# DLRM tower with CIN: the G product once a chunk, in four row quarters and four PSUM banks, with the work for the next chunk behind it

## The chip, the cores and the metric

The kernel runs on one core of a Trainium2 chip. The metric is the device time of the launch in microseconds, as the median of several runs.

## What is computed

39 embeddings of 16 numbers are picked for each of 512 samples; a compressed interaction network of three layers with 128 maps each runs on them; the sums of the three layers over the 16 numbers (z1, z2, z3) and a dense context go through a small MLP.

```python
def _cin_layer(X0, Xi, W, b):                     # X0 (512, 39, 16), Xi (512, Fi, 16)
    Wr = W.reshape(H, F0_, Fi)                    # H = 128
    return jnp.einsum('hjk,bjd,bkd->bhd', Wr, X0, Xi) + b[None, :, None]
X0 = embedded_features; Xi = X0; res = []
for W, b in Ws:                                   # three layers
    Xi = _cin_layer(X0, Xi, W, b)
    res.append(Xi.sum(axis=2))
z = jnp.concatenate(res, axis=1)
...
h = jnp.concatenate([z, dense_ctx], axis=1)
h = jnp.maximum(h @ W_top1 + b_top1, 0.0)
h = jnp.maximum(h @ W_top2 + b_top2, 0.0)
y = h @ W_top3
```

Of the third layer only the sum over d is needed. The kernel therefore forms G[k, j, b] = sum over d of X2[b, k, d] X0[b, j, d] for each sample, and layer 2 becomes 39 matmuls over G.

## The kernel before

The 8192 columns (sample, d) are worked off in 16 **chunks** of 512 columns (32 samples); a chunk has four **blocks** of 128 columns (8 samples). The engines run programs of their own, tied by semaphores, and each loops over chunks (`body`). Places in a chunk are written (i, g): block i, and g the group on PE (0 to 9), the place a among the six groups of ACT, or the place d among the four of DVE.

- **Layer 0** for chunk n + 1 runs in chunk n. SP loads shifted copies of x (`load_x`), ACT copies the rows to a PSUM bank (`store_rows`, rows_ps), DVE forms seven `products` (L481), and PE multiplies them by w0 into quad_ps (`layer0`, L630, seven times). ACT and DVE split the result into a high and a low half, x1_hi and x1_lo. PE also transposes x to xt (`transposes`, L634), in the same bank quad_ps.
- **Layer 1** (`layer1`, L679) has ten groups a block, each of four fields (group 9 of three) and three matmuls: 128 rows against 512 (or 384) columns. Groups 1, 4, 6, 9 go to two banks d_ps and are multiplied by xt and added up by DVE (L538). Groups 0, 2, 3, 5, 7, 8 go to three banks a_ps in turn and are scaled by ACT into `parts` (L902), which POOL adds pairwise (L303). DVE reduces what is left to x2t, the block of X2 with (sample, d) in the partitions (L550).
- **G** (`g_block`, L720): x2t of a block (128 rows) times `diag`, in which x stands on a block diagonal, one 40-column stripe for each of the block's 8 samples (39 fields and a column of ones, which gives z2). The result, 320 columns in g_ps, is copied by ACT to g_sb and z (`store_g`, L911, L912). diag is written by 16 DMAs a chunk from xt (`copy_diag`, L414), and by DVE for chunk 0 (L503).
- **Layer 2** (`layer2`, L733) runs in three parts over the stored G: in chunk 8, in chunk 15 and at the end. Then the MLP (L817, L826, L843, L848).

POOL also gathers the embeddings of chunks n + 2 and n + 3 (L277); SP writes them to x_rows (`write_x`, L373).

The order on each engine is written out by hand in tables of places. On PE, for example:

```python
L0_AT = {(1, 5): 0, (1, 7): 1, (2, 1): 2, (2, 3): 3, (2, 5): 4, (2, 8): 5, (3, 0): 6}
G_AT, STORE_G_AT = {(1, 9): 0, (2, 9): 1, (3, 9): 2}, {(1, 5): 0, (2, 5): 1, (3, 5): 2}
LAST_G_AT, STORE_LAST_G_AT = (1, 1), (1, 0)
```

G of block i is made behind group 9 of block i + 1, that of block 3 behind (1, 1) of the next chunk. Waits of G, of the transposes and of layer 0 are put on the second and third matmul of the layer 1 group ahead of them. Chunk 1 (`LATE`) and the chunks with a part of layer 2 (`PART_AT`) have tables of their own.

Of the kernel before, what the change touches and what calls it, by code (L numbers as in the profile page):

```python
# [24 lines left out]
CB = CW // D  # L25
# [3 lines left out]
BLKS = CW // 128  # L29

# [51 lines left out]
REDUCE_AT, FIRST_REDUCE_AT = 1, 2  # L82
HIGH_X1_AT, LOW_X1_AT, SUM_X1_AT, BIAS_Z1_AT = (3, 0), (3, 1), (0, 0), (1, 2)
PART_HIGH_X1_AT, PART_LOW_X1_AT = (3, 2), (3, 2)
LATE_HIGH_X1_AT, LATE_LOW_X1_AT = (3, 2), (3, 2)
PRODUCTS_AT = {(0, 3): (0,), (1, 0): (1,), (1, 2): (2,), (1, 3): (3,), (2, 0): (4, 5), (2, 2): (6,)}
LATE_PRODUCTS_AT = {(1, 0): (0,), (1, 2): (1, 2), (1, 3): (3,), (2, 0): (4,), (2, 2): (5,), (2, 3): (6,)}
FIRST_TILES = 4

ROWS_AT, LATE_ROWS_AT = (0, 5), (1, 0)  # L90
LATE = (1,)
# [5 lines left out]
FIRST_G_AT, FIRST_STORE_G_AT = {(2, 6): 0, (3, 2): 1, (3, 9): 2}, {(2, 4): 0, (3, 1): 1, (3, 5): 2}  # L97
# [29 lines left out]


def is_late(n):
    return isinstance(n, int) and n in LATE  # L130

# [10 lines left out]
def build(nc, picks0, picks, tables, x_first, x_rows, w0a, w0b, w1, w2, biases, b1_row, ctx_in, wt1, wt1c, bt1, wt2, bt2, wt3,  # L142
          ident_in, mask_in, out):
    with ExitStack() as stack:
# [32 lines left out]
        mask = sb("mask", [128, BLK_B])  # L177
# [31 lines left out]
        a_ps = [ps(f"a_ps{r}") for r in range(A_RING)]  # L209

# [19 lines left out]
        diag_copied = [sem("diag_copied_first"), sem("diag_copied_second")]  # L230
# [4 lines left out]
        g_ready, g_stored = sem("g_ready"), sem("g_stored")  # L235
# [105 lines left out]
        def _(sp):  # L341
# [96 lines left out]
            def body(n, u, w2_at=None, loading=True, writing=True):  # L438
                copy_diag(n, u, 0)
                copy_diag(n, u, 1)  # L440
# [8 lines left out]
            write_x(3, 0)  # L449
            body(1, 1, (0, W2_FIRST))  # L450
# [20 lines left out]
        def _(dve):  # L471
# [69 lines left out]
            def reduce_parts(n, i):  # L541
# [5 lines left out]
                if not (isinstance(q, int) and q < 2):  # L547

                    dve.wait_ge(g_ready, q - 1)
                nc.vector.tensor_reduce(x2t[:, i % 2, :], left[:, :, :], AX_X, ALU.add).then_inc(x2t_ready, 1)  # L550
# [17 lines left out]

            def body(n, u, last=False):
                late = is_late(n)  # L570
                low_x1_at = (PART_LOW_X1_AT if isinstance(n, int) and n in PART_AT else
                             LATE_LOW_X1_AT if late else LOW_X1_AT)
                products_at = LATE_PRODUCTS_AT if late else PRODUCTS_AT
                for i in range(BLKS):
                    for d in range(ND):
                        add_group(n, u, i, d)
                        if d == (FIRST_REDUCE_AT if i == 0 and isinstance(n, int) and n == 1 else REDUCE_AT):
# [8 lines left out]
                        if (i, d) == low_x1_at and not last:  # L586
                            low_x1(n + 1, 1 - u)
                        if not last:
                            for t in products_at.get((i, d), ()):
# [33 lines left out]
            reduce_parts(CHUNKS - 1, BLKS - 1)  # L623

        @block.tensor
        def _(pe):
# [31 lines left out]
            def layer1(n, u, i, g, transposing=False, starting=False, ending=False, g_of=None):  # L658
# [12 lines left out]
                else:  # L671
# [3 lines left out]
                    if a >= A_RING or not is_zero(q):  # L675
# [12 lines left out]
                elif g_of:  # L688

                    if is_zero(g_of[0]):  # L690
                        pe.wait_ge(first_diag, g_of[1] + 1)
                    else:
                        pe.wait_ge(diag_copied[g_of[1] // 2], 16 * BLK_B * g_of[0])
# [7 lines left out]
                if g_of:  # L701
# [367 lines left out]
```

## Time and profile before

| | before |
|---|---|
| time, median of 3 runs (lowest, highest) | 676.58 us (675.15, 676.62) |
| profiled execution | 681.37 us |
| its span, first to last instruction | 679.5 us |
| PE matmul busy / weight loads busy | 655.2 us (96%) / 480.9 us (71%) |
| DVE, ACT, POOL busy | 455.2 (67%), 478.7 (70%), 497.0 us (73%) |
| mean granted TensorE clock | 0.985 |

Busy is the union of an engine's instructions. Matmuls overlap one another in the records, so what one costs is read from the chain of waits, where each piece is the time from one start to the next. PE is TensorE's matmuls, PEld its weight loads. An fp32 matmul has two records and two loads; a transpose and an fp32r matmul have one. The clock is given as a share of 2.4 GHz.

### The profile page before, as it was taken

The page shows a single profiled execution, that of the slowest core. Times are in us where ns is not written, and L with a number is a line of the kernel's source. Part 1 is how long each engine was busy: PE and PEld are TensorE (multiplying, and loading weights), DVE is VectorE, ACT ScalarE, POOL GpSimd, SP SyncE. Part 2 cuts the span into 40 slices and gives each one's busy share as a digit, 9 for nine tenths or more (in the row PEclk, how much of TensorE's full clock was granted, in tenths as well). Part 3 has the DMA queues.
Part 4 walks back from the last instruction along what each step waited for, and adds up shares of the span by engine and source line. Part 5 has one row for each costly group of instructions (what it writes and reads, how often), then busy time and mean ns, then how long its engine had stood idle before and what let it go on. Part 6 is the DMA issues. An engine that isn't in the chain of part 4 may idle for free.

```text
span 679.5 us, 11233 instructions
## 1 busy us (share of the span) xinstructions
PE 655.2 (96%) x2680; PEld 480.9 (71%) x2680; DVE 455.2 (67%) x1180; ACT 478.7 (70%) x1735; POOL 497.0 (73%) x467
## 2 busy tenths in 40 slices
PE   3699989999999999999999999999999999999998
PEld 1386757777777777777787777777777777788563
DVE  1477757878686969687707677878686969674600
ACT  1466758878787879696907878878787879685502
POOL 5888967979797979888826797979797966563500
PEclk9989989999999999999999999999999999999889
DMA  6652514141514233241500515151413232002000
GB/s 157 150 112 54 120 26 116 33 122 13 121 32 104 49 90 61 61 92 39 114 6 5 116 13 118 13 118 13 111 18 90 39 67 57 4 4 83 1 1 0
DMA packets 68134, 43.18 MB, mean 64 GB/s; under 512 B 49418, under 2 KB 61645, under 8 KB 66329
## 3 DMA queue, kind: packets, MB, share of 16 engines
q1 hardware_dynamic: 56742, 37.91, 24.7%
q0 software_dynamic: 5184, 1.29, 2.3%
q10 hardware_dynamic: 6158, 3.45, 1.9%
q8 instruction: 15, 0.25, 0.2%
q14 instruction: 35, 0.29, 0.2%
HBM read 39.45 MB, written 1.96 MB: 61 GB/s over the span
## 4 chain that ended last, share of the span: by engine, by line
PE 88%; issue 3%; POOL 3%; DMA 2%; SPq 2%; DVE 1%; ACT 1%; POOLq 0%; ACTq 0%
PE a_ps L679 37%; PE d_ps L679 23%; PE quad_ps L630 12%; PE quad_ps L733 5%; PE g_ps L720 5%; POOL emb L277 1%; PE d_ps L817 1%; PE a_ps L843 1%; DMA emb<-tables_dram,rows_now 1%; DMA rows<-x_first 1%; POOL left L303 1%; PE quad_ps L634 1%; PE quad_ps L647 1%; SPq L414 1%; POOL parts L303 1%
## 5 line engine op out<-in xcount | busy, mean ns | idle before, releaser
L902 ACT ACTIVATE parts<-a_ps,xt 128x128 f32<-128x128 f32 x1536 | 423.3, 381 | 130.2 <-PE a_ps L679 116.6
L538 DVE SCALAR_TENSOR_TENSOR parts<-d_ps,xt,parts 128x128 f32<-128x128 f32 x704 | 201.7, 343 | 112.5 <-PE d_ps L679 104.6
L303 POOL TENSOR_TENSOR parts<-parts 128x512 f32<-128x512 f32 x128 | 163.4, 1294 | 103.3 <-ACT parts L902 102.5
L679 PE MATMUL a_ps<-w_hi,x_hi 128*128 128x512 f32 x384 | 181.7, 473 | 0.6 <-issue 0.6
L303 POOL TENSOR_TENSOR left<-parts 128x512 f32<-128x512 f32 x128 | 167.1, 1321 | 5.7 <-ACT parts L902 4.0
L277 POOL DMA_INDIRECT emb<-tables_dram,rows_now x150 | 144.2, 961 | 25.3 <-issue 18.8
L679 PE MATMUL a_ps<-w_hi,x_lo 128*128 128x512 f32 x384 | 152.5, 397 | 0.6 <-issue 0.6
L679 PE MATMUL a_ps<-w_lo,x_hi 128*128 128x512 f32 x384 | 151.7, 395 | 0.0
L679 PE MATMUL d_ps<-w_hi,x_hi 128*128 128x512 f32 (+1 forms) x256 | 126.5, 494 | 0.0
L630 PE MATMUL quad_ps<-products,w_sb 117*128 117x512 f32 (+1 forms) x210 | 107.8, 594 | 0.0
L679 PE MATMUL d_ps<-w_lo,x_hi 128*128 128x512 f32 (+1 forms) x256 | 97.7, 382 | 2.8 <-DMA diag<-xt 2.1
L679 PE MATMUL d_ps<-w_hi,x_lo 128*128 128x512 f32 (+1 forms) x256 | 97.2, 380 | 0.0
L550 DVE TENSOR_REDUCE x2t<-left 128x128 f32<-128x1280 f32 x64 | 94.6, 1477 | 2.1 <-POOL left L303 1.6
L679 PEld LDWEIGHTS a_ps<-w_hi,x_hi 128*128 128x128 f32 x384 | 72.5, 189 | 26.2 <-issue 8.7
L679 PEld LDWEIGHTS a_ps<-w_lo,x_hi 128*128 128x128 f32 x384 | 72.7, 189 | 24.5 <-issue 8.1
L679 PEld LDWEIGHTS a_ps<-w_hi,x_lo 128*128 128x128 f32 x384 | 72.5, 189 | 18.8 <-issue 1.2
L481 DVE TENSOR_TENSOR products<-shifted,rows_ps 117x512 f32<-117x512 f32 x105 | 70.2, 682 | 3.1 <-ACT rows_ps L890 3.1
L679 PEld LDWEIGHTS d_ps<-w_lo,x_hi 128*128 128x128 f32 x256 | 48.4, 189 | 28.3 <-issue 17.1
L679 PEld LDWEIGHTS d_ps<-w_hi,x_hi 128*128 128x128 f32 x256 | 48.2, 188 | 27.0 <-issue 11.9
L679 PEld LDWEIGHTS d_ps<-w_hi,x_lo 128*128 128x128 f32 x256 | 48.1, 188 | 8.5
L538 DVE SCALAR_TENSOR_TENSOR parts<-d_ps,xt,b_rows 128x128 f32<-128x128 f32 x64 | 22.4, 350 | 39.4 <-PE d_ps L679 27.8
L630 PEld LDWEIGHTS quad_ps<-products,w_sb 117*128 117x128 f32 (+1 forms) x210 | 40.1, 191 | 9.3
(67 smaller groups left out, 432.2 us busy)
## 6 DMA issues: line engine op xcount, KB each, us to landing
shifted<-x_rows SPq DMA_DIRECT2D x45, 312.0 KB
shifted<-x_rows SPq DMA_DIRECT2D x45, 234.0 KB
diag<-xt SPq DMA_DIRECT2D x240, 4.9 KB
rows<-x_rows SPq DMA_DIRECT2D x45, 78.0 KB
emb<-tables_dram,rows_now POOLq DMA_INDIRECT x150
w_sb<-w_dram SPq DMA_DIRECT2D x6, 384.0 KB
shifted<-x_first SPq DMA_DIRECT2D x12, 136.5 KB
g_sb<-w_dram ACTq DMA_DIRECT2D x2, 768.0 KB, 8.8
```

The source lines that it names most:

```text
L277: nc.gpsimd.indirect_dma_start(out=emb[0:parts, buf, g, :], out_offset=None, in_=tables[:, :], in_offset=bass.IndirectOffsetOnAxis(ap=rows ...
L303: nc.gpsimd.tensor_tensor(to, parts[:, i % 2, now:now + GF, :], parts[:, i % 2, more:more + GF, :], ALU.add).then_inc(pool_added, 1)
L414: sp.dma_start(diag[rows, blks, b, 0:FIELDS], xt[rows, u, blks, :]).then_inc(diag_copied[pair], 16)
L481: nc.vector.tensor_tensor(products[0:PK, t, :], shifted[0:PK, t, :], rows_ps[0:PK, :], ALU.mult).then_inc(products_ready, 1)
L538: nc.vector.scalar_tensor_tensor(now, d_ps[d % D_RING][:, H * at:H * (at + 1)], xt[:, u, i, j:j + 1], before, ALU.mult, ALU.add).then_inc( ...
L550: nc.vector.tensor_reduce(x2t[:, i % 2, :], left[:, :, :], AX_X, ALU.add).then_inc(x2t_ready, 1)
L630: nc.tensor.matmul(quad_ps[:, :], w0_sb[0:rows, t, :], products[0:rows, t, :], start=(t == 0), stop=(t == QT - 1)).then_inc(products_used, 1)
L634: return nc.tensor.transpose(bank[:, FIELDS * i:FIELDS * (i + 1)], rows3[0:FIELDS, 128 * i:128 * (i + 1)], ident[:, :])
L679: return nc.tensor.matmul(bank[:, 0:H * len(fields)], x[:, u, 128 * i:128 * (i + 1)], w[:, fields[0]:fields[-1] + 1, :].rearrange("p j h - ...
L720: nc.tensor.matmul(g_ps[:, 0:(FIELDS + 1) * BLK_B], x2t[:, i % 2, :], diag[:, i, :, :].rearrange("p b j -> p (b j)"), start=True, stop=Tru ...
L733: mm = nc.tensor.matmul(z3_ps[:, 0:(c1 - c0) * CB], w2_sb[:, j, :], g_sb[:, j, c0 * CB - base:c1 * CB - base], start=(j == 0), stop=(j == ...
L902: last = nc.scalar.activation(parts[:, i % 2, 2 + GF * a + at, :], a_ps[(NA * i + a) % A_RING][:, H * at:H * (at + 1)], ACT.Copy, scale=xt ...
```

## The change

G is made once a chunk, in the next chunk behind group (1, 0), for all four blocks (`make_g`). Each block's matmul of 128 rows and 320 columns becomes four of 32 rows and 80 columns: a quarter of 32 rows holds two samples, so only their two stripes of diag are needed, and diag shrinks from 8 to 2 stripes. Quarter r goes to a bank of its own: g_ps, quad_ps, rows_ps, a_ps1. The last is also one of layer 1's three banks, and group (1, 2) waits until it is copied. x2t is kept for four blocks. ACT copies quarters 1 and 2, DVE 3 and 0, each for the whole chunk; z2 is taken out of g_sb by one copy for each half of the samples. As quad_ps and rows_ps now hold G for a while, the rows, the transposes, the products and layer 0 move behind it. The tables for chunk 1 and for the chunks with layer 2 are gone. SP copies diag with 8 DMAs a chunk, and in chunk 1 before the write of chunk 3's first half. At the end the MLP uses d_ps0, d_ps1, a_ps0, a_ps2 instead of rows_ps, d_ps0, d_ps1, a_ps0.

```diff
+TILES = 4
+TILE_P = 128 // TILES
+TILE_B = BLK_B // TILES
-L0_AT = {(1, 5): 0, (1, 7): 1, (2, 1): 2, (2, 3): 3, (2, 5): 4, (2, 8): 5, (3, 0): 6}
-TRANSPOSE_AT, LATE_TRANSPOSE_AT = (0, 9), (1, 2)
-G_AT, STORE_G_AT = {(1, 9): 0, (2, 9): 1, (3, 9): 2}, {(1, 5): 0, (2, 5): 1, (3, 5): 2}
-LAST_G_AT, STORE_LAST_G_AT = (1, 1), (1, 0)
+L0_AT = {(1, 8): 0, (2, 0): 1, (2, 1): 2, (2, 3): 3, (2, 6): 4, (2, 9): 5, (3, 1): 6}
+TRANSPOSE_AT, STORE_XT_AT = (1, 3), (1, 1)
+LAYER2_AT, STORE_Z3_AT = (1, 6), (1, 3)
+G_AT, STORE_G_AT, VECTOR_STORE_G_AT = (1, 0), {(0, 5): 1, (1, 0): 2}, {(0, 3): (3, 0)}
+BEHIND_G = (1, 2)
+REDUCE_AT, FIRST_REDUCE_AT = 0, 2
+HIGH_X1_AT, LOW_X1_AT, SUM_X1_AT, BIAS_Z1_AT = (3, 1), (3, 2), (0, 0), (1, 2)
+PRODUCTS_AT = {(1, 1): (0,), (1, 2): (1, 2), (1, 3): (3,), (2, 0): (4,), (2, 1): (5,), (2, 2): (6,)}
+ROWS_AT = (1, 1)
...
+        g_banks = [g_ps, quad_ps, rows_ps, a_ps[1]]
+        def g_made(r):
+            return g_banks[r][:, 0:BLKS * TILE_B * (FIELDS + 1)].rearrange("p (i b j) -> p j i b", i=BLKS, b=TILE_B)
+        def g_kept(n, r):
+            kept = g_sb[:, :, n * CB % HB:n * CB % HB + CB]
+            return kept.rearrange("p j (i r b) -> p j i r b", i=BLKS, r=TILES)[:, :, :, r, :]
...
+            def copy_diag(n, u):
+                sp.wait_ge(xt_ready, transposed_now)
+                sp.wait_ge(g_ready, taken_before)
+                    sp.dma_start(diag[rows, :, b % TILE_B, 0:FIELDS], xt[rows, u, :, :]).then_inc(diag_copied, 16)
...
-            write_x(3, 0)
-            body(1, 1, (0, W2_FIRST))
+            body(1, 1, (0, W2_FIRST), first=True)
...
-                    if a >= A_RING or not is_zero(q):
+                    if (i, g) == BEHIND_G and not is_zero(n):
+                        pe.wait_ge(vector_stored, 2 * n - 1)
+                    elif a >= A_RING or not is_zero(q):
                         pe.wait_ge(staged_ready, NA * q + a - A_RING + 1)
...
-            def g_block(n, i):
-                q = BLKS * n + i
-                pe.wait_ge(x2t_ready, q + 1)
-                nc.tensor.matmul(g_ps[:, 0:(FIELDS + 1) * BLK_B], x2t[:, i % 2, :],
-                                 diag[:, i, :, :].rearrange("p b j -> p (b j)"),
-                                 start=True, stop=True).then_inc(g_ready, 1)
+            def make_g(n):
+                for i in range(BLKS):
+                    for r in range(TILES):
+                        rows, at = slice(TILE_P * r, TILE_P * (r + 1)), TILE_B * (FIELDS + 1) * i
+                        if i == 0 and r == 0:
+                            pe.wait_ge(x2t_ready, BLKS * (n + 1))
...
+                        mm = nc.tensor.matmul(g_banks[r][:, at:at + TILE_B * (FIELDS + 1)], x2t[rows, i, :],
+                                              diag[rows, i, :, :].rearrange("p b j -> p (b j)"), start=True, stop=True)
+                mm.then_inc(g_ready, 1)
...
-            banks = [rows_ps, d_ps[0], d_ps[1], a_ps[0]]
+            banks = [d_ps[0], d_ps[1], a_ps[0], a_ps[2]]
-                if mt == 1:
+                if mt == 0:
                     pe.wait_ge(vector_added, NDF * (last_q + 1))
-                elif mt == 3:
+                elif mt == 2:
                     pe.wait_ge(staged_ready, NA * (last_q + 1))
...
+            def store_g(n, r):
+                act.wait_ge(g_ready, n + 1)
+                nc.scalar.copy(g_kept(n, r), g_made(r)).then_inc(g_stored, 1)
```

Two places in the order of instructions. First TensorE's around (1, 0) and (1, 1) of chunk 9 (the first is chunk 0); before, one G (of block 3 of the chunk before) stood behind (1, 1), and the transposes ahead of (1, 0):

```order
799 L634 MATMUL quad_ps<-ident,rows 128x39 x4
800 L679 MATMUL a_ps<-w_hi,x_hi 128x512
801 L679 MATMUL a_ps<-w_lo,x_hi 128x512
802 L679 MATMUL a_ps<-w_hi,x_lo 128x512
803 L679 MATMUL d_ps<-w_hi,x_hi 128x512
804 L679 MATMUL d_ps<-w_lo,x_hi 128x512
805 L679 MATMUL d_ps<-w_hi,x_lo 128x512
806 L720 MATMUL g_ps<-diag,x2t 128x320
```

In the changed kernel the same place, behind group (1, 0), whose last row stands first here, holds four rounds over the four banks, rows 848 to 863, and then group (1, 1) from row 864. The first round and the start of the second:

```order
847 L693 MATMUL a_ps<-w_hi,x_lo 128x512
848 L750 MATMUL g_ps<-diag,x2t 128x80
849 L750 MATMUL quad_ps<-diag,x2t 128x80
850 L750 MATMUL rows_ps<-diag,x2t 128x80
851 L750 MATMUL a_ps<-diag,x2t 128x80
852 L750 MATMUL g_ps<-diag,x2t 128x80
853 L750 MATMUL quad_ps<-diag,x2t 128x80
```

So one matmul of 320 columns here, and three more elsewhere in the chunk, have become sixteen of 80 in one place, and the four transposes stand three groups further on.

Then ScalarE's in an ordinary chunk, from its rows copy behind (0, 5) to G of block 1, before:

```order
106 L890 COPY rows_ps<-rows 117x512
107 L902 ACTIVATE parts<-a_ps,xt 128x128 x4
108 L880 COPY xt<-quad_ps 128x156
109 L911 COPY g_sb<-g_ps 128x39x8
110 L912 COPY z<-g_ps 128x8
111 L902 ACTIVATE parts<-a_ps,xt 128x128 x20
112 L911 COPY g_sb<-g_ps 128x39x8
113 L912 COPY z<-g_ps 128x8
```

and in the changed kernel, from the groups up to (0, 5) to the xt copy behind (1, 1):

```order
74 L927 ACTIVATE parts<-a_ps,xt 128x128 x40
75 L937 COPY g_sb<-quad_ps 128x40x4x2
76 L927 ACTIVATE parts<-a_ps,xt 128x128 x4
77 L937 COPY g_sb<-rows_ps 128x40x4x2
78 L927 ACTIVATE parts<-a_ps,xt 128x128 x4
79 L915 COPY rows_ps<-rows 117x512
80 L904 COPY xt<-quad_ps 128x156
```

ACT's copies of G now come as two, a group apart, and the copies of rows and xt stand behind them.

## Rows read from the trace of the kernel before

**Rows 1.** Stretches: us, busy us (and instructions) of each engine, clock, DMA.

```profile
core 0: us, PE busy (x) PEld busy (x) DVE busy (x) ACT busy (x) POOL busy (x), PEclk, DMA share, GB/s
90.00:95.00 5.00, 3.17 (x8) 2.48 (x9) 2.13 (x6) 1.27 (x6) 4.65 (x5) 0.72 0.09 10
138.00:174.00 36.00, 36.00 (x148) 26.83 (x147) 27.96 (x75) 29.17 (x108) 30.68 (x30) 1.00 0.33 74
642.00:647.00 5.00, 5.00 (x6) 1.00 (x4) 0.17 (x1) 0.00 (x0) 0.00 (x0) 0.50 0.00 0
```

**Rows 2.** Chain of waits in mid-kernel: start us, us, what (x records).

```profile
141.90 0.54 PE g_ps L720 x2
...
157.45 0.37 PE quad_ps L634 x4
157.82 0.90 PE a_ps L679 x3
...
162.03 0.70 PE a_ps L679 x3
162.73 0.86 PE quad_ps L630 x2
...
166.55 0.53 PE d_ps L679 x3
...
193.78 0.89 PE a_ps L679 x3
```

**Rows 3.** Waits of PE from 33 us on: us in total, times, longest.

```profile
PE d_ps L679 <- DMA diag<-xt: 2.1, 1, 2.1
```

**Rows 4.** Groups of instructions: busy us, mean ns of one, idle before.

```profile
L720 PE MATMUL g_ps<-diag,x2t 128*128 128x320 f32 x128 | 45.9, 441 | 0.0
...
L902 ACT ACTIVATE parts<-a_ps,xt 128x128 f32<-128x128 f32 x1536 | 423.3, 381 | 130.2 <-PE a_ps L679 116.6 <-issue 11.5
L911 ACT COPY g_sb<-g_ps 128x312 f32<-128x312 f32 x64 | 29.0, 453 | 22.7 <-PE g_ps L720 22.6
...
L817 PEld LDWEIGHTS rows_ps<-z,shifted 128*128 128x128 f32 x6 | 1.0, 190 | 1.2 <-issue 1.2
...
L826 PEld LDWEIGHTS rows_ps<-shifted 16*128 16x128 f32 x2 | 0.3, 182 | 0.4 <-issue 0.4
```

**Rows 5.** Chain of waits: two parts of layer 2, and the end.

```profile
340.44 17.07 PE quad_ps L733 x78
...
608.96 8.71 PE quad_ps L733 x78
...
638.33 1.05 PE rows_ps L826 x2
...
651.20 1.02 PE g_ps L720 x2
```

**Rows 6.** Timeline of weight loads: start us, us to the last end.

```profile
84.21 0.19 PEld L679 LDWEIGHTS a_ps<-w_hi,x_hi 128*128 128x128 f32 x1
84.32 0.19 PEld L679 LDWEIGHTS a_ps<-w_lo,x_hi 128*128 128x128 f32 x1
...
157.38 0.26 PEld L634 LDWEIGHTS quad_ps<-ident,rows 39*128 39x128 f32 x3 [0.24 <-issue]
157.38 0.32 PEld L634 LDWEIGHTS quad_ps<-ident,rows 39*128 39x128 f32 x4 [0.24 <-issue]
```

**Rows 7.** Timeline of ACT in an ordinary chunk.

```profile
142.48 0.42 ACT L911 COPY g_sb<-g_ps 128x312 f32<-128x312 f32 x1 [0.45 <-PE g_ps L720]
...
158.28 0.65 ACT L890 COPY rows_ps<-rows 117x512 f32<-117x512 f32 x1
```

**Rows 8.** Timeline of SP, PE, PEld and DVE: chunk 1, and the last adds.

```profile
85.26 9.08 SPq L414 DMA_DIRECT2D diag<-xt  x14
91.83 0.45 PE L679 MATMUL d_ps<-w_lo,x_hi 128*128 128x384 f32 x1 [2.13 <-DMA diag<-xt]
96.01 0.19 PEld L679 LDWEIGHTS d_ps<-w_lo,x_hi 128*128 128x128 f32 x1 [0.24 <-issue]
...
638.36 0.71 DVE L538 SCALAR_TENSOR_TENSOR left<-d_ps,xt,parts 128x128 f32<-128x128 f32 x2
```

More of the change, by code:

```diff
@@ L126 @@
 W1_PART_AT = {0: 0, 3: 1, 6: 2}
-def is_late(n):
-    return isinstance(n, int) and n in LATE
 def is_zero(count):
@@ L546, in reduce_parts @@
                 dve.wait_ge(pool_added, ADDS * (q + 1))
-                if not (isinstance(q, int) and q < 2):
-                    dve.wait_ge(g_ready, q - 1)
-                nc.vector.tensor_reduce(x2t[:, i % 2, :], left[:, :, :], AX_X, ALU.add).then_inc(x2t_ready, 1)
+                if not is_zero(n):
+                    dve.wait_ge(g_ready, n)
+                nc.vector.tensor_reduce(x2t[:, i, :], left[:, :, :], AX_X, ALU.add).then_inc(x2t_ready, 1)
             def first_body():
@@ L567, in first_body @@
                             multiply_l0(1, t)
+            def store_g(n, r):
+                dve.wait_ge(g_ready, n + 1)
+                if n == HALF_CHUNKS:
+                    dve.wait_ge(z2_ready, 1)
+                nc.vector.tensor_copy(g_kept(n, r), g_made(r)).then_inc(vector_stored, 1)
             def body(n, u, last=False):
[L570 to L573, printed above, removed]
                 for i in range(BLKS):
@@ L585, in body @@
                                                     ).then_inc(z1_biased, 1)
-                        if (i, d) == low_x1_at and not last:
+                        for r in VECTOR_STORE_G_AT.get((i, d), ()):
+                            store_g(n - 1, r)
+                        if (i, d) == LOW_X1_AT and not last:
                             low_x1(n + 1, 1 - u)
                         if not last:
-                            for t in products_at.get((i, d), ()):
+                            for t in PRODUCTS_AT.get((i, d), ()):
                                 multiply_l0(n + 1, t)
@@ L623, in _ @@
             reduce_parts(CHUNKS - 1, BLKS - 1)
+            for r in (3, 0):
+                store_g(CHUNKS - 1, r)
         @block.tensor
@@ L931, in first_body, with body @@
                             store_xt(1, 1)
-                        if (i, a) in FIRST_STORE_G_AT:
-                            act.wait_ge(w1_lo_ready, 3)
-                            store_g(0, FIRST_STORE_G_AT[i, a], 0)
                         if (i, a) == SECOND_HIGH_X1_AT:
                             high_x1(1, 1)
-            def body(n, u, half, last=False, half_before=None):
+            def body(n, u, last=False):
                 part = PART_AT.get(n) if isinstance(n, int) else None
-                late = is_late(n)
-                high_x1_at = PART_HIGH_X1_AT if part is not None else LATE_HIGH_X1_AT if late else HIGH_X1_AT
                 for i in range(BLKS):
@@ L990, in _ @@
             first_body()
-            body(1, 1, 0)
-            for n in range(2, HALF_CHUNKS):
-                body(n, n % 2, 0)
-            body(HALF_CHUNKS, 0, 1, half_before=0)
-            body(HALF_CHUNKS + 1, 1, 1)
-            for n in range(HALF_CHUNKS + 2, CHUNKS - 2):
-                body(n, n % 2, 1)
-            body(CHUNKS - 2, 0, 1)
-            body(CHUNKS - 1, 1, 1, last=True)
-            store_g(CHUNKS - 1, BLKS - 1, 1)
+            for n in range(1, CHUNKS):
+                body(n, n % 2, last=n == CHUNKS - 1)
+            for r in (1, 2):
+                store_g(CHUNKS - 1, r)
+            store_z2(1)
             store_z3(2)
-            banks = [rows_ps, d_ps[0], d_ps[1], a_ps[0]]
+            banks = [d_ps[0], d_ps[1], a_ps[0], a_ps[2]]
             for mt in range(N1 // 128):
@@ L1008, in _ @@
                 act.wait_ge(mlp_ready, N1 // 128 + mt + 1)
-                nc.scalar.activation(h2[:, mt, :], a_ps[1 + mt][:, :], ACT.Relu, bias=bt2_sb[:, mt:mt + 1]
+                nc.scalar.activation(h2[:, mt, :], (a_ps[1], rows_ps)[mt][:, :], ACT.Relu, bias=bt2_sb[:, mt:mt + 1]
                                      ).then_inc(mlp_stored, 1)
```

150 lines of the change are left out of this document (71 added, 79 removed).

## Prediction

> **What bounds the kernel now.** I read the page's busy shares first: PE stands far above the other engines. Then the table of stretches, which shows PE busy for 36.00 of 36.00 us between 138 and 174 us at the full granted clock [rows 1], and the chain of waits, where the same point of two chunks lies 35.96 us apart (157.82 and 193.78) [rows 2]. The pieces of the chain add up to that by themselves: 36 groups of layer 1 at 0.70, 4 narrow ones at 0.53, seven products of layer 0 at 0.86, four G at 0.54 and the transposes, thus 25.2 + 2.1 + 6.0 + 2.2 + 0.6 = 36.1. So TensorE waits for nobody in an ordinary chunk, and a change is worth there what it does to PE's own time. The list of waits confirms it: in the chunks PE's longest wait is 2.1 us on the copy into diag, in chunk 1 [rows 3]. ACT and DVE have slack, but little: 29 and 28 of 36 us are filled [rows 1].
>
> **The change, part by part.** The sum is made on the profiled execution: 681.37 us, span 679.5. The median of the three timed runs is 676.58, 4.8 less. I take the difference found here off the median.
>
> *1. G itself.* Now: four matmuls of 128 rows and 320 columns, 0.54 us each, 2.16 us a chunk [rows 2]. Each is two records, with a weight load in each (128 records for 64 G) [rows 4]. New: 16 matmuls of 32 rows and 80 columns, so 32 loads and 32 matmul records. In columns nothing is saved, as 16 x 80 = 4 x 320. Only what runs at once can save, and no row of this trace shows two row quarters at work together. The bounds:
>
> - Streams. Layer 2 takes 17.07 us for 78 records of 256 columns and 8.71 for 78 of 128 [rows 5]: 0.219 and 0.112 us a record, 0.84 ns a column. 80 columns are 0.067 us, an instruction (two records) 0.133. All four quarters at once: 16 x 0.133 / 4 = 0.53 us. If only neighbouring instructions overlap, since the second record of one must follow its first in the same rows: 16 x 0.067 = 1.07.
> - Loads. Two full loads follow each other by 0.11 us (84.21, 84.32), the transposes' loads by 0.06 (a fourth one lengthens the piece from 0.26 to 0.32) [rows 6]. Fewer rows make a load no shorter: 182 ns for 16 rows, 190 for 128 [rows 4]. Loads in neighbouring quarters side by side: 16 x 0.112 = 1.79 us. All one behind the other: 32 x 0.112 = 3.58.
> - Changing the height of the array. The 16-row and 128-row matmuls that alternate after the last chunk take 1.05 us apiece at full clock [rows 5], layer 0's of the same 512 columns 0.86 [rows 2]: 0.19 a change. The transposes (39 rows) add 0.37 and stretch the next group from 0.70 to 0.90 [rows 2], 0.57 in all; less four load distances of 0.06 that leaves 0.33 for two changes. I take 0.35 for the two around G.
>
> I choose half way between the two neighbour bounds, 1.43 us, because the two records of an instruction must share their rows, and no row says whether streams or loads then set the pace; with 0.35 for the changes that is 1.78 us. Against 2.16 it is -0.38 a chunk, 16 chunks: **-6.1 us**. The ends are 0.53 + 0.35 = 0.88 (-20.5 us) and 3.58 + 0.35 = 3.93 (+28.3 us).
>
> The row above says that 16 rows load as slowly as 128. The Trainium skill has the same rule (TensorE: Matmul & The Clock Gate, "LDWEIGHTS (loading the stationary operand)"): a load costs its columns, not its rows. By that rule alone, with loads one by one, this change loses; that is the first rival. The skill's TensorEngine Tiling (Array Packing), "Tiling Modes", speaks for it: tiles load and multiply independently, and a change of mode drains the engine. No run here shows the first half yet; the 0.19 us of the rows agrees with the second. The first page's "Packing small matmuls — row/col tiling" also gives a measured 3.07x for four row quarters, an estimate of 2.16 / 3.07 = 0.70 us plus the changes.
>
> *2. G's copies.* Before: eight a chunk on ACT, the four large ones 453 ns in the mean [rows 4]. New: two on ACT and two on DVE of 320 elements, 0.45 to 0.5 us each. Both are covered by PE's work while they keep up, so they cost nothing themselves. The tight places, from T, the end of group 9 in block 0: (1, 0) ends at T + 0.70, G at T + 2.48. DVE empties a_ps1 first, by about T + 3.03; PE wants that bank for group (1, 2) at T + 3.18. ACT (four scaled copies of a group 1.10 us, 423.3 / 1536 x 4 [rows 4]; a copy of G began 0.04 us after its matmul, 141.90 + 0.54 [rows 2, 7]) does quadrant 1, group (1, 0), quadrant 2, group (1, 1), rows (0.65 [rows 7]), the short xt, group (1, 2), and is free at about T + 7.8; PE wants that bank for (1, 8) at T + 2.48 + 7 x 0.70 + 0.57 = T + 7.95. With so little room I allow 0.05 us a chunk, **+0.8**. After it, layer 0's own pieces of 0.86 us on PE give both engines time to catch up.
>
> *3. Order.* Transposes, rows, products and layer 0 come later in the chunk, in the same number, so PE gains or loses nothing. On SP the diag copies are 8 rather than 16 a chunk, and its loads of x are freed as before by the products of block 2 and meet a later user: no cost.
>
> *4. Chunk 1.* Before, SP has the write of x_rows for chunk 3, which waits for gathers, ahead of the diag copies; they start at 85.26, and PE waits 2.13 us for them in (1, 9) [rows 8]. Behind that wait the granted clock reads 0.72 [rows 1]; from 91.83 to 96.01 [rows 8] PE did what at full clock costs 2.44 us (0.35 + 0.53 + 0.70 + 0.86), a loss of 1.7. New: G of chunk 1 is wanted only in chunk 2, and the copies are issued before that write: **-3.8**. The smaller multiplies into diag in chunk 0 may bring a little more; I count nothing.
>
> *5. The end.* The first bank of the last layers is now d_ps0, which waits for DVE's last adds, over at 638.36 + 0.71 = 639.07 [rows 8], where rows_ps began at 638.33 [rows 5]: **+0.8**. The last G is four blocks behind the half-clock stretch (0.50) [rows 1], where one block cost 1.02 [rows 5]: streams and loads double, 2 x 1.43 + 0.35 = 3.21 against the 1.78 of part 1, less the 0.48 that the one block already lost: **+0.9**. Two large copies an engine rather than a large and a small one: **+0.3**.
>
> Sum: -6.1 + 0.8 - 3.8 + 0.8 + 0.9 + 0.3 = **-7.1 us**, thus 676.6 - 7.1 = **669.5 us**.
>
> **The rivals.** Parts 2 to 5 alone are -1.0; each rival adds its own G.
>
> - *Loads one after another (slower).* For it: loads cost by columns, and no row has two at once. Against: nothing in this trace. 3.93 a chunk: +28.3 - 1.0, 704 us. It decides once a load and its matmul take over (2.16 - 0.35) / 32 = 0.057 us on average; the full ones have 0.112.
> - *Break-even.* Quarters don't overlap, but their loads run at the transposes' 0.06: 32 x 0.06 + 0.35 = 2.3, +2.3 us; or the neighbour bound of loads holds, 1.79 + 0.35 = 2.14, -0.3 us. 675 to 678 us.
> - *All four quarters at once.* 0.88 us: -20.5 - 1.0, 655 us. Against: the two records of one instruction share their rows.
> - *A new stall or a lower clock.* ACT or DVE late by 0.5 us a chunk at (1, 2) or (1, 8) takes back 8 us: 677.5. Or a G of few rows makes the granted clock fall, as it had fallen by 642 us in matmuls that alternate 16 and 128 rows: at the 1.7 us of part 4, 16 times, +27, 697 us.
>
> **Numbers.** Partial overlap as forecast 0.38 (660 to 673 us), all at once 0.12, break-even 0.24, loads one by one 0.18, stall or clock 0.08. Within 0.3% (2 us) is what a measurement of this kernel can't tell from no change; of break-even half lies in there and a quarter on each side. Faster 0.38 + 0.12 + 0.06 + 0.01 = 0.57, same 0.12, slower 0.06 + 0.18 + 0.07 = 0.31. The range takes in 655, and above it the stalls and loads that overlap only in part: 654 to 698, leaving out most of the first rival.
>
> **What would show it.** Sixteen matmuls of 80 columns between (1, 0) and (1, 1), whose piece in the chain is 1.4 to 2.0 us, so that two records start within 0.06 us of each other on average; a chunk every 35.4 to 35.8 us; no wait of PE on diag; PE idle about 1.3 us before the last layers. Records 0.11 us apart and a chunk of 37.7 us mean the first rival. I am wrong too if PE waits at (1, 2) or (1, 8), or if the granted clock falls in mid-kernel.

## The result: 7.6% slower, and the profile after

The changed kernel takes 727.83 us (median of 4, 726.53 to 729.4), the kernel before 676.6 in the same session. The ratio is 1.076 with a 95% interval of 1.0719 to 1.0801. The forecast was 669.5 us with a range of 654 to 698. In some executions of a kernel, of before too, its last layers run at half clock for 10 to 20 us, in others not; that moves a time by some 9 us (e1 below took 679.1 us at a mean clock of 1.00 and 688.4 at 0.98), so I compare chunks as well as medians.

The page of the profiled execution (engines, and the slices in which the span is cut in 40):

```profile
span 724.6 us, 11784 instructions
PE 667.0 (92%) x3064; PEld 490.8 (68%) x3064; DVE 471.3 (65%) x1212; ACT 461.2 (64%) x1641; POOL 496.1 (68%) x467
PEclk9899999999989898989989989898998989999999
PE 44%; POOL 21%; issue 20%; ACT 8%; DVE 4%; DMA 1%; SPq 1%; POOLq 1%; DVEq 0%
```

TensorE's busy share is high, as before, but the last line, the chain by engine, says that it is no longer the bound by itself: POOL has 21% of the chain. And the granted clock dips again and again in mid-kernel. The stretches (columns as in [rows 1]) of two whole chunks, from one G to the next, and of the time right behind a G:

```profile
120.18:158.20 38.02, 35.34 (x174) 26.11 (x174) 28.90 (x77) 27.76 (x101) 30.59 (x30) 1.00 0.32 70
196.22:237.25 41.03, 38.35 (x175) 28.43 (x174) 28.95 (x77) 28.06 (x101) 30.60 (x30) 0.92 0.30 63
197.00:203.00 6.00, 6.00 (x38) 4.45 (x35) 3.41 (x7) 3.52 (x12) 2.73 (x3) 0.50 0.08 12
```

A chunk was 35.96 us [rows 2]. It is 38.02 now where the clock stays at 1.00, with 2.68 us in which PE is idle, and 41.03 where 6 us run at half clock. The waits between 100 and 650 us (us in total, times, longest):

```profile
POOL parts L309 <- ACT parts L927: 117.3, 56, 4.5
ACT g_sb L937 <- PE a_ps L750: 56.6, 13, 4.9
DVE x2t L555 <- POOL left L309: 47.4, 23, 3.2
PE d_ps L693 <- DVE parts L543: 32.5, 13, 2.7
```

The first two are idle time of engines that aren't the bound. The last two belong together, as the timelines of POOL, DVE and PE at the start of a chunk show:

```profile
185.17 1.29 POOL L309 TENSOR_TENSOR parts<-parts 128x512 f32<-128x512 f32 x1
186.61 0.96 POOL L283 DMA_INDIRECT emb<-tables_dram,rows_now  x1
187.59 1.32 POOL L309 TENSOR_TENSOR left<-parts 128x512 f32<-128x512 f32 x1
189.06 0.96 POOL L283 DMA_INDIRECT emb<-tables_dram,rows_now  x1 [0.15 <-issue]
190.03 1.32 POOL L309 TENSOR_TENSOR left<-parts 128x512 f32<-128x512 f32 x1
...
191.55 1.49 DVE L555 TENSOR_REDUCE x2t<-left 128x128 f32<-128x1280 f32 x1 [3.22 <-POOL left L309]
192.96 0.68 DVE L517 TENSOR_REDUCE z<-quad_ps 128x32 f32<-128x512 f32 x1
193.55 2.41 DVE L543 SCALAR_TENSOR_TENSOR parts<-d_ps,xt,parts 128x128 f32<-128x128 f32 x9
...
194.72 0.44 PE L693 MATMUL d_ps<-w_hi,x_hi 128*128 128x384 f32 x1 [2.68 <-DVE parts L543]
```

In the chunk's block 0, DVE comes to the reduce of the block before already behind its first group (REDUCE_AT = 0, before 1). It needs POOL's last add of that block, which ends at 191.35, because gathers of 0.96 us stand between the adds. DVE waits 3.22 us, and with it the adds that empty d_ps; PE waits 2.68 us for a bank at (0, 9). Then the clock falls. The same place in the timeline of the kernel before, which I had not looked at:

```profile
153.77 1.32 POOL L303 TENSOR_TENSOR left<-parts 128x512 f32<-128x512 f32 x1
...
153.13 0.68 DVE L512 TENSOR_REDUCE z<-quad_ps 128x32 f32<-128x512 f32 x1
154.17 1.13 DVE L538 SCALAR_TENSOR_TENSOR parts<-d_ps,xt,parts 128x128 f32<-128x128 f32 x4 [0.36 <-PE d_ps L679]
155.30 1.49 DVE L550 TENSOR_REDUCE x2t<-left 128x128 f32<-128x1280 f32 x1
```

POOL's add ends at 155.09, and the reduce begins at 155.30, in time by 0.2 us. Its new place is where `sum_x1` begins, at 153.13, 2.0 us too early.

G is the small thing that I argued most about. Its first matmuls (at half clock here):

```profile
196.15 0.50 PE L750 MATMUL g_ps<-diag,x2t 32*128 32x80 f32 x1
196.16 0.50 PE L750 MATMUL quad_ps<-diag,x2t 32*128 32x80 f32 x1
196.16 0.50 PE L750 MATMUL rows_ps<-diag,x2t 32*128 32x80 f32 x1
196.17 0.50 PE L750 MATMUL a_ps<-diag,x2t 32*128 32x80 f32 x1
196.44 0.42 PE L750 MATMUL g_ps<-diag,x2t 32*128 32x80 f32 x1
```

All four quarters start within 0.02 us: they do run at once. The starts of G near the end are a test that the kernel makes by itself. POOL's last gather starts at 598.1 us, so no gather stands between its adds of block 3 in chunks 13 and 14:

```profile
582.40 0.42 PE g_ps L750
...
620.87 0.26 PE g_ps L750
...
656.55 0.26 PE g_ps L750
```

The two stretches are 38.47 us and 35.68, where those before took 41.03. PE's wait at (0, 9) is 0.32 us at the end of each, and not 2.68; the first stretch still begins with a fall of the clock (0.57 from 581 to 589), behind the last long wait.

### The profile page after: what moved, and what is told of

It reads as the page before. It is cut to its first block, busy times and chain, and to the rows that moved or that the text cites. A ratio compares the mean times of both kernels' runs of the same rounds, so it can differ in the third digit from the quotient of the medians.

```text
span 724.6 us, 11784 instructions
## 1 busy us (share of the span) xinstructions
PE 667.0 (92%) x3064; PEld 490.8 (68%) x3064; DVE 471.3 (65%) x1212; ACT 461.2 (64%) x1641; POOL 496.1 (68%) x467
## 4 chain that ended last, share of the span: by engine, by line
PE 44%; POOL 21%; issue 20%; ACT 8%; DVE 4%; DMA 1%; SPq 1%; POOLq 1%; DVEq 0%
PE a_ps L693 15%; PE d_ps L693 11%; POOL left L309 9%; ACT parts L927 7%; POOL emb L283 6%; POOL parts L309 5%; PE quad_ps L764 5%; PE quad_ps L642 4%; PE g_ps L750 3%; DVE parts L543 2%; DVE z L517 1%; PE quad_ps L646 1%; PE d_ps L842 1%; PE a_ps L842 1%; DMA rows<-x_first 1%
## 5 line engine op out<-in xcount | busy, mean ns | idle before, releaser
L693 PE MATMUL a_ps<-w_hi,x_lo 128*128 128x512 f32 x384 | 157.4, 410 | 1.4 <-DVE x_lo L512 1.2
L693 PE MATMUL a_ps<-w_lo,x_hi 128*128 128x512 f32 x384 | 156.4, 407 | 0.0
L693 PE MATMUL d_ps<-w_hi,x_hi 128*128 128x512 f32 (+1 forms) x256 | 123.7, 483 | 32.8 <-DVE parts L543 32.8
L693 PE MATMUL d_ps<-w_lo,x_hi 128*128 128x512 f32 (+1 forms) x256 | 100.0, 391 | 0.2 <-ACT xt L904 0.2
L693 PE MATMUL d_ps<-w_hi,x_lo 128*128 128x512 f32 (+1 forms) x256 | 99.8, 390 | 0.0
L693 PEld LDWEIGHTS a_ps<-w_hi,x_hi 128*128 128x128 f32 x384 | 75.2, 196 | 29.5 <-issue 15.2
L693 PEld LDWEIGHTS a_ps<-w_lo,x_hi 128*128 128x128 f32 x384 | 75.3, 196 | 27.3 <-issue 14.7
L693 PEld LDWEIGHTS a_ps<-w_hi,x_lo 128*128 128x128 f32 x384 | 75.2, 196 | 20.1 <-DVE x_lo L512 1.6
L937 ACT COPY g_sb<-quad_ps 128x320 f32<-128x320 f32 x16 | 7.2, 453 | 69.0 <-PE a_ps L750 69.0
```

Source lines behind the costliest of these rows:

```text
L693: return nc.tensor.matmul(bank[:, 0:H * len(fields)], x[:, u, 128 * i:128 * (i + 1)], w[:, fields[0]:fields[-1] + 1, :].rearrange("p j h - ...
```

## The experiments

Theory R: the reduce, moved ahead of POOL's adds, makes the stall and the stall makes the clock fall. Its rival: the many small matmuls of G make the clock fall, or ACT waiting for them makes the stall; the expectations call it C, and G in e8. The table has all runs; "chunk" is the time between the same places of two chunks in mid-kernel (G, or the transposes where G is the old one) in the profiled execution. The ratio is to the kernel before as it ran in the same session.

| run | reduce behind group | two gathers of block 3 | else | chunk, us | median, us | ratio to before |
|---|---|---|---|---|---|---|
| before | 1 | in block 3 | | 35.96 | 676.6 | |
| changed | 0 | in block 3 | | 41.03, first 38.02 | 727.83 | 1.076 |
| e1 | 1 | in block 3 | | 36.53 | 688.12 | 1.014 |
| e3 | 1 in block 0, else 0 | in block 3 | | 36.85 | 688.12 | 1.016 |
| e5 | 1 | in block 3 | product 0 first | 36.09 | 681.76 | 1.006 |
| e6 | 1 | in block 3 | x1_lo earlier | 36.30 | 684.85 | 1.012 |
| e7 | 1 | in block 3 | both | 35.86 | 677.51 | 1.000 |
| e8 | 0 | end of block 2 | | 35.78 | 678.03 | 1.000 |
| e9 | 1 in block 0, else 0 | end of block 2 | | 35.07 | 667.79 | 0.980 |
| e10 | 1, block 3: 2 | end of block 2 | both, banks at the end | 35.29 | 670.24 | 0.984 |
| e4 | 1 | in block 3 | quarters in a row | 38.05, three 39.5 | 717.06 | 1.062 |
| e2 (before) | 0 | in block 3 | | 37.77, two 39.3 | 701.52 | 1.040 |
| e11 (before) | 1 | end of block 2 | | 35.96 | 675.5 | 0.993 |
| e12 (before) | 0 | end of block 2 | | 35.95 | 675.22 | 0.995 |

**e1, the reduce back.** The changed kernel with

```diff
-REDUCE_AT, FIRST_REDUCE_AT = 0, 2
+REDUCE_AT, FIRST_REDUCE_AT = 1, 2
```

> The changed kernel with DVE's reduce back behind its second group (REDUCE_AT = 1), all else as changed. Theory R (the early reduce holds DVE for POOL's last add, DVE keeps the d_ps banks, PE stalls at (0, 9) and its clock falls): no wait of PE on DVE, granted clock at 1.00 in mid-kernel, a chunk every 35 us, time 655 to 668 us. Rival C (the clock and the stall come from G itself: four banks held and ACT waiting 4 us a chunk for it): the stall stays or moves to (1, 2) or (1, 8), the clock still falls around G, time above 700 us. Rival P (POOL is too late whatever DVE does): PE still waits 1 to 2 us a chunk, 680 to 700 us.

Measured: 688.12 us (679.1 to 689.16), ratio 1.0139 (1.0087 to 1.0191). One number gives back 40 of the 51 us, and the clock, with G unchanged:

```profile
191.35:227.88 36.53, 35.61 (x174) 26.03 (x174) 28.56 (x76) 28.00 (x103) 30.55 (x30) 1.00 0.34 71
```

So the same G without the stall leaves the clock at 1.00: in this kernel the fall comes with the stall. The chunk is 4.50 us shorter, 1.49 of it at full clock (38.02 - 36.53) and 3.01 of it clock. But my theory was too hopeful: it said 655 to 668. The chunk is 36.53, above before. The time lies in the range of rival P, but PE doesn't wait for POOL, and DVE waits for it only 5.9 us in all. What is left shows in two waits of PE on DVE, one a chunk each:

```profile
PE a_ps L693 <- DVE x_lo L512: 7.2, 14, 0.5
PE quad_ps L642 <- DVE products L486: 4.9, 12, 0.4
```

**e2, the early reduce alone, in the kernel before** (REDUCE_AT = 0, nothing else).

> The kernel before with only the reduce moved ahead, behind DVE's first group (REDUCE_AT = 0). Theory R: the same DVE wait for POOL in block 0, PE waits 1 to 3 us a chunk on DVE and the clock falls, time 700 to 730 us. Rival C: with G as before nothing happens, 674 to 682 us.

Measured: 701.52 us, ratio 1.0403 (1.0344 to 1.0461). Half of the damage, with the old G. The chunk is 1.81 us longer than before at full clock (37.77 - 35.96), about as much as the stall costs in the changed kernel (1.49 against e1). What is missing is the clock: it was to fall in general, and it fell in two chunks, behind two of twelve waits of 1.5 to 1.6 us. PE waits 1.6 us at most instead of 2.7; the second fence is one of the two falls:

```profile
DVE x2t L550 <- POOL left L303: 33.9, 35, 2.1
PE d_ps L679 <- DVE parts L538: 18.6, 12, 1.6
```

```profile
121.00:126.00 5.00, 5.00 (x17) 3.81 (x18) 3.73 (x10) 2.01 (x8) 4.17 (x4) 0.66 0.12 13
```

**e3, the reduce back in block 0 only.**

```diff
-                        if d == (FIRST_REDUCE_AT if i == 0 and n == 1 else REDUCE_AT):
+                        if d == (FIRST_REDUCE_AT if i == 0 and n == 1 else 1 if i == 0 else REDUCE_AT):
```

> The changed kernel with the reduce moved back in block 0 of each chunk alone, which is the reduce of the block 3 before. Theory R in its narrow form (only that reduce meets POOL late, since POOL has gathers behind three adds of block 3): the same time as with all four moved back, within 2 us. Its wide form (every block's reduce is early): 5 us or more above it. Rival C: above 700 us.

Measured: 688.12 us, ratio 1.0158 (1.0078 to 1.0237), as e1. The stall at (0, 9) is gone with one reduce moved back, as the narrow form said. But the equal median isn't an equal kernel: the chunk is 36.85 against 36.53, DVE still waits for POOL 44.8 us, in 36 waits, almost three a chunk, and PE waits for the products 12.9 us. The lateness had moved, not gone.

**e4, the quarters in a row.** e1 with the loops of `make_g` exchanged, so that four matmuls in the same quarter follow each other.

```diff
-                for i in range(BLKS):
-                    for r in range(TILES):
+                for r in range(TILES):
+                    for i in range(BLKS):
```

> Reduce moved back, and the sixteen matmuls of G in the other order: all four blocks of quarter 0, then of quarter 1 and so on, so that neighbours share their 32 rows. If the four quarters run at once in the changed order (as its trace looks, eight rounds of 0.21 us at half clock), this order loses it: G takes 2.2 to 4 us instead of about 1.3, 15 to 40 us more than with the reduce alone moved back. If rounds were quick for another reason (short streams, cheap loads), the same time within 2 us.

Measured: 717.06 us, ratio 1.0619 (1.058 to 1.0658), 29 more than e1. The same 16 matmuls take 2.62 us, from 197.33 to 199.95, where in e1 they take 1.06, and the ordinary chunk is 1.52 us longer (38.05 against 36.53). The quarters don't run wholly one by one: each starts 0.51 us behind the last, which then has several records left, and the eight records of a quarter start 0.11 us apart. So the gain of e1's order lies in the alternation of the quarters.

Three chunks take 39.5 us instead of 38.05, because the clock falls behind G, in the first of them here:

```profile
161.00:165.00 4.00, 4.00 (x14) 2.81 (x13) 1.45 (x5) 3.46 (x13) 2.52 (x3) 0.57 0.11 15
```

No wait of PE in mid-kernel is longer than 0.53 us in this run. So the clock can fall without a long stall. That speaks for my rival that a G of few rows brings it down, for G in this order; in the changed kernel's order G leaves it at 1.00 in e1, e8 and e9.

**e5, e6, e7: the two waits left in e1.** All three start from e1. e5 puts the first product ahead of the reduce in block 1, e6 x1_lo one group earlier, e7 does both.

```diff
-PRODUCTS_AT = {(1, 1): (0,), (1, 2): (1, 2), (1, 3): (3,), (2, 0): (4,), (2, 1): (5,), (2, 2): (6,)}
+PRODUCTS_AT = {(1, 2): (1, 2), (1, 3): (3,), (2, 0): (4,), (2, 1): (5,), (2, 2): (6,)}
...
+                        if (i, d) == (1, 1) and not last:
+                            multiply_l0(n + 1, 0)
                         if d == (FIRST_REDUCE_AT if i == 0 and n == 1 else REDUCE_AT):
...
-HIGH_X1_AT, LOW_X1_AT, SUM_X1_AT, BIAS_Z1_AT = (3, 1), (3, 2), (0, 0), (1, 2)
+HIGH_X1_AT, LOW_X1_AT, SUM_X1_AT, BIAS_Z1_AT = (3, 1), (3, 1), (0, 0), (1, 2)
```

> The changed kernel with the reduce back behind the second group (as in the run reduce back), and in block 1 DVE makes the first of layer 0's products ahead of that reduce instead of behind it; nothing else. Theory W (what is left against the kernel before is made of two waits of PE on DVE a chunk, each because the reduce of 1.47 us now stands right ahead of a result that PE has no slack for): the first wait, of layer 0's first matmul at (1, 8), goes, PE quad_ps <- DVE products falls from 4.9 us to under 1 in 100 to 650, the chunk goes from 36.54 us to about 35.8, and the time from 688 to about 677. Rival H (PE's waits are only where a general lateness shows, since the products and the reduce are the same work in either order): the wait moves to d_ps or to the next product, and the time stays within 3 us of 688.

> The changed kernel with the reduce back behind the second group, and x1_lo of the next chunk one group earlier on DVE, at (3, 1) behind the reduce, where it stood in the kernel before; nothing else. Theory W: the second wait, of the third matmul of the next chunk on x1_lo, goes (PE a_ps <- DVE x_lo 7.2 us to 0 in 100 to 650, 0.5 to 0.7 us a chunk with what PE loses around it), the time falls by 7 to 10 us to about 680. Rival H: DVE's group (3, 2) is then later by 0.75 us, PE waits there for a bank of d_ps instead, and the time stays within 3 us of 688.

> Both edits of the two runs before it together: first product ahead of the reduce in block 1, and x1_lo at (3, 1). Theory W: the chunk is that of the kernel before less what G saves, 35.96 - 0.9 = 35.05 us, so 14 chunks give 12 to 13 us and chunk 1's wait on diag 4 more, less some us for the end of the kernel: 660 to 670, faster than the kernel before. Rival H: within 3 us of 688. Rival P (another bound stands close behind, that of DVE's adds or ACT's copies of G): between, 672 to 680, with new waits of PE on DVE parts or ACT parts.

Measured: 681.76, 684.85 and 677.51 us, ratios 1.006 (1.0012 to 1.0107), 1.0115 (1.0052 to 1.0179) and 1.0003 (0.9956 to 1.0051); the chunk goes from 36.53 to 36.09, 36.30 and 35.86. The savings add up (0.44 + 0.23 = 0.67), so the waits are two separate ones, each smaller than I had expected (0.7 and 0.5 to 0.7). e7 is rival P's case: a new wait stands close behind. It is there in e6 already, where rival H had it, with the same 4.0 us: the wait for x1_lo of 7.2 us is gone, and only 0.23 us a chunk is won.

```profile
PE d_ps L695 <- DVE parts L543: 4.0, 14, 0.3
```

**e8, the gathers early.** The changed kernel as it is, with

```diff
-GATHER_AT = (..., (2, 1), (2, 3), (3, 1), (3, 2), (3, 3))
+GATHER_AT = (..., (2, 1), (2, 3), (2, 3), (2, 3), (3, 3))
```

> The changed kernel as it is, the reduce behind the first group, with POOL's two gathers between its adds of block 3 moved to the end of block 2, where POOL idles 2.4 us for ACT; nothing else. Theory R (DVE's early reduce meets POOL's last add of block 3, and the adds are late because gathers of 0.98 us stand between them; PE's wait for a d_ps bank and the fallen clock follow from it): POOL ends those adds 1.9 us earlier, DVE x2t <- POOL falls from 47 us to under 25 in 100 to 650, PE's wait at (0, 9) from 2.7 to about 0.7 us a chunk, the clock of mid-kernel rises from 0.92, and the time falls from 728 to 695 to 710. Rival G (the clock falls because of G's 16 small matmuls, and DVE waits at all places alike): the clock stays at 0.92 to 0.95, and the time falls by under 10 us.

Measured: 678.03 us (669.65 to 678.58), ratio 1.0000 (0.9959 to 1.0042). One line of POOL's order takes 50 us off the changed kernel, more than the 18 to 33 that I expected. Now POOL issues three gathers in the time that it idled, and its adds follow each other:

```profile
178.58 0.94 POOL L283 DMA_INDIRECT emb<-tables_dram,rows_now  x1 [0.30 <-issue]
179.53 2.55 POOL L309 TENSOR_TENSOR parts<-parts 128x512 f32<-128x512 f32 x2
182.04 2.56 POOL L309 TENSOR_TENSOR left<-parts 128x512 f32<-128x512 f32 x2
...
184.80 1.49 DVE L555 TENSOR_REDUCE x2t<-left 128x128 f32<-128x1280 f32 x1 [0.99 <-POOL left L309]
```

```profile
189.47:225.25 35.78, 35.33 (x175) 26.10 (x174) 28.93 (x77) 27.76 (x101) 30.45 (x30) 1.00 0.34 74
```

The second fence is the stretch of a chunk. DVE's wait of 3.22 us is 0.99 (27.6 us in all, not under 25), PE's of 2.68 is 0.5 at most, and the clock no longer falls in mid-kernel, with G as it was.

**e9, gathers early and the reduce of block 0 back.** Both edits, of e8 and of e3.

> The changed kernel with POOL's two gathers moved to the end of block 2 (as in the run gathers early) and, in block 0 alone, the reduce behind the second group. Theory R2 (what waits in the run gathers early, 0.5 us a chunk of PE at (0, 9) with 0.2 to 0.3 around it, comes from block 0, where DVE waits for POOL 1.3 us and then has the reduce and sum_x1 ahead of its second group): that wait goes, the chunk goes from 35.78 to about 35.2 us, the time from 678 to about 670. Rival D (the reduce at (0, 1) pushes DVE's product 0 at (1, 1), as it did without the gathers' move): PE quad_ps <- DVE products comes back with over 5 us in 100 to 650, and the time is 675 to 685.

Measured: 667.79 us (666.05 to 668.47), ratio 0.9801 (0.9709 to 0.9894). This beats both kernels, and by theory R2's numbers; rival D's wait for the products isn't there. PE works without a gap, and the chunk is what G alone should make of it, 35.96 - 0.90 = 35.06 (the 0.90 is worked out from the pieces of the chain further down). The stretch of a chunk, and in a second fence the start of it in the chain (the rest of G's rounds left out):

```profile
185.76:220.84 35.08, 35.08 (x175) 26.19 (x174) 28.82 (x76) 27.82 (x103) 30.52 (x30) 1.00 0.35 74
```

```profile
185.76 0.26 PE g_ps L750
...
186.82 0.90 PE d_ps L693 x3
187.72 1.40 PE a_ps L693 x6
...
220.84 0.26 PE g_ps L750
```

**e10, the other way there.** e7 with the gathers early, block 3's reduce one group later still, and at the end ACT's two banks ahead of DVE's two.

```diff
-                        if d == (FIRST_REDUCE_AT if i == 0 and n == 1 else REDUCE_AT):
+                        if d == (FIRST_REDUCE_AT if i == 0 and n == 1 else 2 if i == 3 else REDUCE_AT):
...
-            banks = [d_ps[0], d_ps[1], a_ps[0], a_ps[2]]
+            banks = [a_ps[0], a_ps[2], d_ps[0], d_ps[1]]
```

> The run with both edits (reduce behind the second group, product 0 ahead of it in block 1, x1_lo at (3, 1)) with three more: POOL's two gathers at the end of block 2, block 3's reduce behind its third group, and at the end of the kernel ACT's two banks taken ahead of DVE's two. Theory W: PE's last waits of the middle (PE d_ps <- DVE parts 4.0 us in 100 to 650) go, the chunk comes near 35.96 - 0.9 = 35.1 us from 35.86, and PE's 4.6 us wait ahead of the last layers becomes about 1 to 2: the time goes from 677.5 to 660 to 667, faster than the kernel before. Rival P (some other engine bounds the chunk near 35.8): the chunk stays at 35.7 to 35.9, and only the end gives 3 us: 674.

Measured: 670.24 us, ratio 0.9838 (0.9746 to 0.9929), chunk 35.29; theory W's time was 660 to 667. The wait on d_ps is gone; 0.22 us more than in e9 stay, and where is open. The 4.6 us that the expectation takes for a wait ahead of the last layers was a misreading: it is the time from where the chain leaves PE to the first of the last layers (635.83 to 640.43 in e1), and for most of it PE still works. PE's wait is 1.3 us in e1 and e7 and 1.1 in e10, so there was little to win.

**e11 and e12, the same order in the kernel before.** e11 moves only the gathers, e12 the gathers and the reduce (to group 0).

> The kernel before with POOL's two gathers at the end of block 2, as a control of the run gathers early. Theory R: POOL is no one's wait in the kernel before (DVE x2t <- POOL 1.6 us in all), so nothing changes: within 2 us of the kernel before. Rival K (the gathers' place is worth something by itself, and the 50 us of that run are not the meeting of reduce and POOL): faster by over 5 us.

> The kernel before with the reduce behind the first group (as in the run before, reduce early, 701.5 us) and POOL's two gathers at the end of block 2. Theory R (an early reduce is dear only where it meets POOL's gathers, whatever G is like): most of the 25 us comes back, DVE x2t <- POOL from 35.6 us to under 15 in 100 to 650, the time from 701.5 to 678 to 685. Rival E (the early reduce is dear by itself, since the adds of POOL end late in any case): 693 to 702.

Measured: 675.5 us for e11, ratio 0.993 (0.9886 to 0.9974). The kernel before had a median of 683.03 beside e9 to e11, with more of its ends at half clock, and 676 to 677 elsewhere; its chunk and that of e11 are the same, so I take this for no gain, and count e9 and e10 against 676 to 677 as 1.0 to 1.4% faster. That is cautious: all times of e9 and e10 have a mean clock of 0.979 to 0.985, and the times of before at such a clock beside them are 681.8 to 685.5 us, which makes them about 2% faster. e12 takes 675.22 us, ratio 0.9952 (0.9917 to 0.9986): with the gathers out of the way, the early reduce that cost 24 us costs nothing. DVE still waits for POOL 17.6 us in all (33.9 in e2; I had expected under 15), but PE no longer waits for DVE. That is the cleanest test of the stall in theory R, since G is the old one; it says little of the clock, which fell only twice in e2.

## Why the prediction was wrong

**The step that failed is part 3, "Order".** It said that transposes, products and layer 0 "come later in the chunk, in the same number, so PE gains or loses nothing". I counted instructions and not the waits between them, and I never looked at two numbers of the diff: REDUCE_AT from 1 to 0, and LOW_X1_AT from (3, 1) to (3, 2) (worth 0.23 us a chunk in e6). The trace of before would have told: POOL's add ended 0.2 us ahead of the reduce that needs it, so a reduce one group earlier had to wait. In the changed kernel that cost, up to the end of layer 1, 686.24 - 618.02 = 68.2 us against e9: a stall of 2.95 us (38.02 - 35.07) in eleven chunks, 32; 3.0 us of lost clock in ten, 30; the remaining 6 stand ahead of chunk 2's G (4.6) and in chunks 13 and 14. That half of it is clock I know from rows (0.92 against 1.00), and that it goes with the stall from e1 and e8. What a stall needs to bring the clock down stays open: the first two of twelve waits of 2.68 us had no fall behind them, two of twelve waits of 1.6 us in e2 had one, and in e4 the clock fell three times with no wait over 0.53.

**Part 1, G, was right in direction and too timid in size.** I took half way between bounds, 1.43 + 0.35 us. The chain of e9 has G at 1.06 (185.76 to 186.82) and 0.20 more in the next group, 1.26 in all, -0.90 a chunk instead of -0.38. The rival "all four quarters at once" (0.88) was right in its mechanism: a round of four starts every 0.11 us at full clock, 0.21 at half. Eight rounds are 0.9, so 0.36 is left for the two changes of height, forecast at 0.35. The 0.11 is the distance of two full loads in [rows 6], not the 0.067 of an 80-column stream, and in e4 the records of one quarter are 0.11 apart as well. So each quarter keeps this pace by itself, and four keep it side by side; that it is the loads that set it I only conclude from the equal distance. The objection that the two records of one matmul share their rows counts for nothing: two records are two rounds. With 32 records / 4 x 0.11 + 0.35 the sum would have been 1.23.

The Trainium skill (TensorEngine Tiling (Array Packing), "Tiling Modes") says that tiles load and multiply in parallel; the runs agree (1.06 us for e1's order, 2.62 for e4's). The Trainium skill's 3.07x for four row quarters (TensorE: Matmul & The Clock Gate, "Packing small matmuls — row/col tiling") isn't reached: 2.16 / 1.06 is 2.04, and 1.7 with the change of height. The two aren't quite the same ratio: its streams have 512 columns, these have 80, and 2.16 is the time of the full-height matmuls. Against the same small matmuls quarter by quarter, which overlap in part, it is 2.62 / 1.06 = 2.5.

**Part 2, the copies**, was right in kind: in the changed kernel and in e9 PE doesn't wait at (1, 8); at (1, 2) PE's loads wait 2.2 us in 14 chunks in e9 for DVE's copy, 0.16 us a chunk, partly under PE's work. So the copies cost between nothing and 2.2 us, against the +0.8 of the sum.

**Part 4, chunk 1**, was right in kind: no wait on diag remains. e9 is through with group (1, 0) of chunk 2 at 115.63, the kernel before at 121.87 + 0.89 = 122.76: 7.1 us ahead. Of that 2.2 are only put off, since before had by then made three G of chunk 1 (1.62) and the transposes (0.57), which e9 makes later. Of the other 4.9 I had forecast 3.8 for the wait and its clock and 0.4 for chunk 0's G, which gave 0.9. The changed kernel is only 2.6 us ahead there, as the first stall stands in between.

**Part 5, the end.** The wait for d_ps0 was forecast at 0.8 and is

```profile
687.37 1.09 PE L851 MATMUL d_ps<-shifted 16*128 16x512 f32 x2 [1.15 <-DVE left L543]
```

1.15 us. The rest depends on the clock: in this execution the last layers run at full clock, and from layer 1's end the kernel takes 36.2 us (686.24 to 722.47) against 39.0 before (638.33 to 677.33); in that of e9, where 620 to 637 stands at 0.51, 45.4. Where the reduce stands matters little here: PE waits 1.28 us at this place in e1 and 1.30 in e7, with the reduce at group 1, and 1.15 in e8 and e9.

**The rivals and the numbers.** The last rival, "ACT or DVE late", had the place wrong and the price far too low: I gave a stall 0.5 us a chunk at (1, 2) or (1, 8), and it was 2.95 us at (0, 9), ahead of the chunk's G and its copies. And I had its two halves as alternatives, a stall or a lower clock, where in this kernel the one came with the other: 2.95 + 3.0 us a chunk is 6, and my highest case had 1.7. The list of what would prove me wrong did name a clock that falls in mid-kernel.

## What to carry to other kernels

When a table of places changes, take each moved instruction and ask what it waits for and by how much the trace has that in time; a margin of 0.2 us is no margin. An engine with a third of its time free (POOL here) can still be late at one place, because of what stands between two of its instructions: moving two gathers of 0.96 us was worth 50 us in the changed kernel, and nothing in the kernel before, where nobody waited for POOL. And a stall of TensorE is to be priced with the clock that it may cost: here as much again for waits of 2.7 us, little for those of 1.6.

## What the hardware showed that I had not expected

- Matmuls of 32 rows in four row quarters start within 0.01 to 0.02 us of each other, with their loads; a round of four with 80 columns takes 0.11 us at full clock and 0.21 at half. The same matmuls quarter by quarter take 2.62 us instead of 1.06, with the records of each quarter still 0.11 us apart.
- After a wait of PE of 2.7 us in a stream of matmuls without gaps, the granted clock was 0.50 from 197 to 203 us, which lost 3.0 us. It came in the chunks from 196 us on and not in the two before, with the same wait. Behind waits of 1.5 to 1.6 us it came in two chunks of twelve (e2), and in e4 three times behind a G of 2.62 us, with no wait over 0.53.
- Whether the last layers run at half clock differs between executions of the same kernel; it moves its time by some 9 us.
